# Two-layer graph network: A's last block by row tiles, W0's scale by slabs, bias added in PSUM, store in three parts

## What is computed

```python
# layer 0
h = jnp.maximum(_layernorm(x), 0.0)
hidden = h @ W0 + b0
x = x + (adj != 0) @ hidden / deg[:, None]     # deg: column sums of adj != 0
# layer 1, 4 heads of 512
h = jnp.maximum(_layernorm(x), 0.0)
ht = (h @ W1) by heads; src, dst = ht @ a_src, ht @ a_dst
e = leaky_relu(src[:, :, None] + dst[:, None, :]) + adj
x = x + (softmax(e) @ ht).mean over heads
```

## Time and profile before

| | us |
|---|---|
| median of 3 runs | 2520.13 (2519.99 to 2520.54) |
| the profiled execution | 2519.26 |
| its span | 2517.5 |
| TensorE busy in it | 2453.3 (97%) |
| VectorE busy | 1878.0 (75%) |
| ScalarE busy | 1260.7 (50%) |

### The profile page before, as it was taken

One profiled execution on the slowest core, in us unless ns is written; L12 is line 12 of the kernel. 1 busy time (PEld: TensorE's weight loads), 2 busy tenths in 40 slices (PEclk: granted clock), 3 DMA queues, 4 the chain that ended last, 5 costly groups with the idle time before them and its releaser, 6 DMA issues.

```text
span 2517.5 us, 42703 instructions
## 1 busy us (share of the span) xinstructions
PE 2453.3 (97%) x12304; PEld 1202.2 (48%) x12304; DVE 1878.0 (75%) x2570; ACT 1260.7 (50%) x1881; POOL 47.6 (2%) x42
## 2 busy tenths in 40 slices
PE   6999999799999999999999999999999999999997
PEld 3444446444444444444444444444444444444785
DVE  7788766776787766877668776687766886767775
ACT  4545645644455444554445544455445554444563
POOL 0000000000000000000000000000000000000000
PEclk9999999799999999999999999999999999999999
DMA  4186647100021000310003000030001200001000
GB/s 146 52 296 193 234 150 247 51 5 5 25 84 46 4 4 25 93 38 4 4 25 96 34 4 4 25 96 34 4 4 33 88 34 3 2 17 44 26 1 9
DMA packets 74148, 144.20 MB, mean 57 GB/s; under 512 B 4414, under 2 KB 11840, under 8 KB 72895
## 3 DMA queue, kind: packets, MB, share of 16 engines
q1 hardware_dynamic: 74047, 143.08, 17.7%
HBM read 129.37 MB, written 13.70 MB: 57 GB/s over the span
## 4 chain that ended last, share of the span: by engine, by line
PE 95%; DVE 2%; ACT 1%; issue 1%; DMA 1%; SPq 0%; ACTq 0%; DVEq 0%
PE z_ps L718 70%; PE o_ps L746 11%; PE z_ps L1326 6%; PE o_ps L1326 4%; PE c_ps L1326 1%; PE c_ps L1358 1%; PE o_ps L1299 1%; PE c_ps L1299 1%; PE o_ps L1350 0%; ACT h_reg L1155 0%; DVE w_reg L1001 0%; DMA row_reg<-b_in 0%; DVE bst L984 0%; PE o_ps L1286 0%; ACT w_reg L1162 0%
## 5 line engine op out<-in xcount | busy, mean ns | idle before, releaser
L718 PE MATMUL z_ps<-hl_reg,h_reg 128*128 (+2 forms) x8736 | 1758.5, 364 | 10.6 <-DVE hl_reg L595 10.6
L718 PEld LDWEIGHTS z_ps<-hl_reg,h_reg 128*128 (+1 forms) x8736 | 855.1, 98 | 910.5 <-DVE hl_reg L595 10.9
L546 ACT ACTIVATE hl_reg<-t_reg (+2 forms) x364 | 361.9, 994 | 729.3 <-DVE t_reg L622 379.3
L595 DVE TENSOR_TENSOR hl_reg<-t_reg,hl_reg (+2 forms) x364 | 417.4, 1147 | 234.5 <-ACT hl_reg L546 232.3
L531 ACT ACTIVATE t_reg<-ring_reg,vv 128x512 f32 (+3 forms) x728 | 526.4, 770 | 67.5 <-DVE ao_reg L610 60.7
L622 DVE SCALAR_TENSOR_TENSOR t_reg<-t_reg,vv,e_reg (+3 forms) x728 | 509.9, 741 | 10.7 <-issue 8.2
L610 DVE TENSOR_TENSOR ao_reg<-ao_reg,t_reg 128x1024 f32<-128x1024 f32 (+1 forms) x336 | 383.4, 1141 | 0.0
L746 PE MATMUL o_ps<-w_reg,z_reg 128*128 128x512 f16 x1248 | 278.2, 379 | 0.9 <-DVE z_reg L638 0.9
L746 PEld LDWEIGHTS o_ps<-w_reg,z_reg 128*128 128x128 f16 x1248 | 119.8, 98 | 140.9 <-DVE z_reg L638 1.2
L638 DVE SCALAR_TENSOR_TENSOR z_reg<-z_ps,z_reg 128x512 f16<-128x512 f32 (+1 forms) x112 | 73.2, 653 | 151.6 <-ACT z_reg L558 151.6
L445 ACT ACTIVATE e_reg<-e_reg (+2 forms) x91 | 90.3, 996 | 153.8 <-DVE e_reg L456 153.5
(11 more groups left out here) (153 smaller groups left out, 1055.2 us busy)
## 6 DMA issues: line engine op xcount, KB each, us to landing
ring_reg<-adjT_in SPq DMA_DIRECT2D x78, 512.0 KB, 4.7
e_reg<-adjT_in SPq DMA_DIRECT2D x78, 512.0 KB, 3.7
ring_reg<-x_in SPq DMA_DIRECT2D x13, 512.0 KB, 4.4
x_dram<-ring_reg SPq DMA_DIRECT2D x13, 512.0 KB, 6.4
ring_reg<-c_dram SPq DMA_DIRECT2D x24, 256.0 KB, 3.3
ao_reg<-x_dram SPq DMA_DIRECT2D x6, 1024.0 KB, 5.5
out_dram<-ao_reg SPq DMA_DIRECT2D x6, 1024.0 KB
w_reg<-W_in SPq DMA_DIRECT2D x5, 1024.0 KB, 6.0
```

What stands on the lines that cost most here:

```text
L546: nc.scalar.activation(hl_ring[:, g % HL_RING, 0, :, 0:W], t_ring[:, g % T_RING, :, 0:W], ACT.Copy).then_inc(hi_ready, 1)
L595: nc.vector.tensor_tensor(hl_ring[:, g % HL_RING, 1, :, 0:W], t_ring[:, g % T_RING, :, 0:W], hl_ring[:, g % HL_RING, 0, :, 0:W], ALU.subtr ...
L718: mm = nc.tensor.matmul(z_ps[:, k, 0:W], hk[hs], hl_ring[:, r, ps, u, 0:W], start=first and u == 0 and n == 0, stop=last and u == 1 and n ...
```

## The change

**Store.** The last block's 128 rows are stored as soon as their sum is done; of the other 127 rows, 112 and 15 are stored apart. **Bias.** b0 times the scale is split in two fp16 halves, high in partitions 0 to 63 and low in 64 to 127 of one tile; a 13th matmul a tile, against a constant tile (b0_one), adds it in PSUM. hid16's halves are made from PSUM; `hidden_sum` and its fp32 buffer go. **W0's scale.** x's first tile is loaded first (group 0 is one tile, the next three), then W0 in four slabs, each with its own maximum; one matmul of ones with the maxima gives every partition their sum, which takes the maximum's place as a scale (SH is 8 times larger for it). The lists of the head are written out anew. **A's last block.** It goes row tile by row tile: 13 pairs for the first row tile, then 13 for the second, and so on, 52 steps of 4 matmuls. All 13 A tiles live to the end of it; row_reg is taken out of the ring. At the steps LN1_AT (6, 8, 10, 11, 13 ... 46) stand one tile's transposes and the scores of the tile before, for 25 tiles; at steps 4, 10 and 16 the last groups of row maxima, at 24 their transposition, all before max_bc is loaded. The block's tiles are groups of two, one and one. Loads of e follow the a_pe counts of the fourth row tile. The fp16 splits of the last two pairs (`high1`, `split1`) stand behind c's transposition.

```diff
+ROW_SLOT = 10
...
+            if g == LAST0:
+                ring = [(r, q) for r, q in ring if r != ROW_SLOT]
...
+        LN1_AT = [math.ceil(6 + 5 * m / 3) for m in range(NT - 1)]
+        LATE_SPLIT = PAIRS - IT // 2
...
+        late_max = [3, 4, 5]
+        LATE_MAX_AT = [4, 10, 16]
+        MR_AT = 24
...
-                           else FULL * H * IT + H * LASTW // P + 2)
+                           else FULL * H * IT + H * LASTW // P + 1)
                 if isinstance(b, int) and b == FULL:
-                    r0 = FULL * BW
-                    sp.dma_start(out[r0:r0 + P, :], out_acc[:, 0]).then_inc(out_st, 16)
-                    sp.dma_start(out[r0 + P:N, :], out_acc[0:LASTP, 1]).then_inc(out_st, 16)
+                    r0, r1 = FULL * BW, FULL * BW + P
+                    sp.dma_start(out[r0:r1, :], out_acc[:, 0]).then_inc(out_st, 16)
+                    sp.wait_ge(o_out, FULL * H * IT + H * LASTW // P + 2)
+                    sp.dma_start(out[r1:r1 + LAST16, :], out_acc[0:LAST16, 1]).then_inc(out_st, 16)
+                    sp.dma_start(out[r1 + LAST16:N, :], out_acc[LAST16:LASTP, 1]).then_inc(out_st, 16)
...
-                sp.dma_start(w0_raw.rearrange("p (k n) -> p k n", k=KT),
-                             W0.rearrange("(k p) n -> p k n", p=P)).then_inc(w0_in, 16)
                 load_x(0)
+                for k in range(KT):
+                    sp.dma_start(w0_raw[:, k * D:(k + 1) * D], W0[k * P:(k + 1) * P, :]).then_inc(w0_in[k], 16)
...
-                for i in range(PAIRS):
+                for i in range(LATE_SPLIT):
                     store_x1(i)
...
-                    if i >= 2:
-                        sp.wait_ge(a_pe, LAST0 + i - 1)
-                        load_e(sp, 0, i - 2)
...
+                sp.wait_ge(mr_sb, 1)
+                sp.dma_start(max_dram.rearrange("(t i) -> t i", i=P), max_st[0:NT]).then_inc(mr_out, 16)
+                sp.wait_ge(mr_out, 16)
+                load_max(sp, 0)
+                for p in range(PAIRS):
                     sp.wait_ge(a_pe, LAST0 + p + 1)
                     load_e(sp, 0, p)
-                sp.wait_ge(mr_sb, 2)
-                sp.dma_start(max_dram[order[-1] * BW:FULL * BW].rearrange("(t i) -> t i", i=P),
-                             max_st[0:IT]).then_inc(mr_out, 16)
+                for i in range(LATE_SPLIT, PAIRS):
+                    store_x1(i)
...
+                def w0_maximum(k):
+                    dve.wait_ge(w0_in[k], 16)
+                    nc.vector.tensor_reduce(w0m[:, k:k + 1], w0_raw[:, k * D:(k + 1) * D], AX_X, ALU.max,
+                                            apply_absolute_value=True).then_inc(s_w0red, 1)
...
+                    dve.wait_ge(s_b0hi, 1)
+                    nc.vector.tensor_tensor(b0_16[P // 2:P], b0_bc[P // 2:P], b0_16[P // 2:P],
+                                            ALU.subtract).then_inc(s_b0lo, 1)
...
-                def hidden_sum(t):
...
-                    nc.vector.tensor_tensor(hid16[:, t, 1], hid32[:, t % 4], hid16[:, t, 0],
-                                            ALU.subtract).then_inc(hid_lo, 1)
+                    if t == NT - 1:
+                        dve.wait_ge(s_lastsc, 1)
+                    nc.vector.scalar_tensor_tensor(out=hid16[:, t, 1], in0=o_ps[:, 2] if t % 2 == 0 else c_ps[:],
+                                                   scalar=SH if t < NT - 1 else last_sc[:], in1=hid16[:, t, 0],
+                                                   op0=ALU.mult, op1=ALU.subtract).then_inc(hid_lo, 1)
...
+                stats0(0)
+                w0_maximum(0)
+                variances0(0)
+                w0_maximum(1)
+                scalars0(0)
+                w0_maximum(2)
+                w0_maximum(3)
+                b0_maximum()
+                stats0(1)
                 w0_scale()
-                for t in range(2, 4):
-                    stats0(t)
-                group0(1)
-                for k in range(KT):
-                    w0_lo(k)
                 b0_scale()
-                dve.wait_ge(s_const, 4)
-                for i in range(NT + 6):
+                transposed_lo(0)
+                w0_lo(0)
+                stats0(2)
+                w0_lo(1)
+                stats0(3)
+                w0_lo(2)
+                w0_lo(3)
...
+                    if c == NG1 - 1:
+                        for p in range(E_PRE0):
+                            subtract_max(dve, 0, p)
+                    for i in range(i0, i1, 2):
+                        for k in range(i, min(i + 2, i1)):
+                            x1_tile(k)
+                        for k in range(i, min(i + 2, i1)):
+                            x1_stats(k)
+                    ln_variances(dve, t0, t1, x1_bst, i1, s_mv1, i1)
+                    while split < min(i0 // 2, LATE_SPLIT):
+                        split1(split)
+                        split += 1
...
+                    act.wait_ge(hid_ps, t + 1)
+                    if t == NT - 1:
+                        act.wait_ge(s_lastsc, 1)
+                    nc.scalar.activation(hid16[:, t, 0], o_ps[:, 2] if t % 2 == 0 else c_ps[:], ACT.Copy,
+                                         scale=SH if t < NT - 1 else last_sc[:]).then_inc(hid_hi, 1)
...
+                def high1(j):
+                    p = pairs1[j]
+                    if j >= LATE_SPLIT:
+                        act.wait_ge(a_pe, NA)
+                    act.wait_ge(st1_ready, 2 * j + 2)
+                    nc.scalar.activation(h16[:, 2 * p:2 * p + 2, 0], ln1_stage[:, j % 2],
+                                         ACT.Copy).then_inc(hi1_done, 1)
...
+                for j in range(LATE_SPLIT, PAIRS):
+                    high1(j)
...
-                    mm.then_inc(hid_ps, 1)
-
-                pe.wait_ge(s_const, 4)
+                            nc.tensor.matmul(bank, ht0[:, t % 3, hs, k], w0_16[:, ws, k],
+                                             start=k == 0 and m == 0, stop=False)
+                    if t == 0:
+                        pe.wait_ge(s_b0lo, 1)
+                    nc.tensor.matmul(bank, b0_one, b0_16, start=False, stop=True).then_inc(hid_ps, 1)
+
+                pe.wait_ge(s_const, 6)
+                transpose0(0)
                 pe.wait_ge(s_w0mx, 1)
-                nc.tensor.transpose(z_ps[0:1, 0, 0:P], w0mx[:], ident[:]).then_inc(w0t_ps, 1)
-                pe.wait_ge(s_w0row, 1)
-                nc.tensor.matmul(z_ps[:, 1, 0:1], w0row, ones32[0:1], start=True, stop=True).then_inc(w0b_ps, 1)
-                for t in range(NT + 2):
+                nc.tensor.matmul(z_ps[:, 0, 0:1], ones_m, w0mx[:], start=True, stop=True).then_inc(w0b_ps, 1)
+                hidden(0)
...
+                def late_step(it, p):
+
+                    g = LAST0 + p
+                    pe.wait_ge(a_ready, g + 1)
+                    a = a_ring[a_slot[g]]
+                    for u in range(2):
+                        for s in range(2):
+                            mm = nc.tensor.matmul(acc0(NB - 1, it), a[:, u, it * P:(it + 1) * P],
+                                                  hid16[:, 2 * p + u, s], start=p == 0 and u == 0 and s == 0,
+                                                  stop=p == PAIRS - 1 and u == 1 and s == 1)
+                    if it == IT - 1:
+                        mm.then_inc(a_pe, 1)
+                    elif p == PAIRS - 1:
+                        mm.then_inc(o_ready, 1)
+
+                pe.wait_ge(o_sb, o_count(NB - 2))
+                for step in range(IT * PAIRS):
+                    late_step(*divmod(step, PAIRS))
+                    for c, at in zip(late_max, LATE_MAX_AT):
+                        if step == at:
+                            pe.wait_ge(o_sb, o_count(NB - 1))
+                            pe.wait_ge(mx_fold, NB)
+                            if c != late_max[0]:
+                                pe.wait_ge(mt_red, len(early_max) + late_max.index(c))
+                            transpose_max(c, o_ps[:, 2])
+                    if step == MR_AT:
+                        max_rows()
+                    for i in range(NT - 1):
+                        if step == LN1_AT[i]:
+                            transpose1(i)
+                            if i > 0:
+                                scores(i - 1)
+                scores(NT - 2)
```

More of the change, by code:

```diff
@@ L18 @@
+import math
 from contextlib import ExitStack
@@ L237, in gnn_kernel @@
         LAST0 = NA - PAIRS
-        groups0 = [(0, 2), (2, 4), (4, 8), (8, 14), (14, 20), (20, NT)]
-        groups1 = [(t, t + IT) for t in range(0, order[-1] * IT, IT)] + [(FULL * IT, NT),
-                                                                         (order[-1] * IT, FULL * IT)]
+        groups0 = [(0, 1), (1, 4), (4, 8), (8, 14), (14, 20), (20, NT)]
+        L0 = order[-1] * IT
+        groups1 = [(t, t + IT) for t in range(0, L0, IT)] + [(FULL * IT, NT), (L0, L0 + 2),
+                                                             (L0 + 2, L0 + 3), (L0 + 3, L0 + 4)]
```

(48 more changed lines are left out.)

207 lines of the change are left out of this document (64 added, 143 removed).

## The result

| | before | after |
|---|---|---|
| median of 4 runs | 2520.06 (2518.62 to 2520.54) | 2495.56 (2493.88 to 2497.17) |
| the profiled execution | 2519.26 | 2494.08 |
| its span | 2517.5 | 2492.3 |
| TensorE busy | 2453.3 | 2447.1 |
| VectorE busy | 1878.0 | 1866.4 |

Times in us. The ratio after to before is 0.9904, with a 95% interval of 0.9886 to 0.9921. Forecast were 2497.5, in a range of 2491 to 2504.

A forecast was written before the change was run, and what follows sets the result against it. The prediction took TensorE as the bound in the hidden features, A's earlier blocks and second layer as untouched. Store -11.8, head and bias -0.6, last block +4.8, behind it -14.7 sum to -22.3: forecast 2497.5 us, range 2491 to 2504.

The forecast's parts named there:

- Store: End of the kernel: 127 rows stored as 112 and 15 use several DMA engines instead of one, -11.8 us.
- Rival B: Last store: the last 15 rows sit on one engine, +3.2 us, 2500.7; chance 7%.
- Bias matmul: Hidden features: one more 512-column matmul a tile at 0.22 us, paid by 24 tiles because TensorE bounds the stage, +5.3 us.
- Head: Start of the kernel: W0's scale is ready earlier, so the fifth tile's transposes start at 29.7 instead of 36.1, -6.2 us.
- rival C: Head gives nothing: b0 or x(1) lands late, or VectorE's longer list eats the gain; +6.2 us, 2503.7; chance 12%.
- A's last block: More transposes, scores and maxima inside the block, and a wait of 1.9 us from 14 ring slots: ends 4.8 us later.
- Rival A: A's last block: the vector chain paces it, six groups give +7 us, 2504.5; chance 15%.
- Rival E: A's last block: TensorE's granted clock falls to 0.50 and stays, all 80 us give 2537; chance 2%.
- Rival D: ScalarE and VectorE quicker behind the block, and no wait of 1.9 us in it: -4 us, 2493.5; chance 10%.
- Behind the block: Between A's last block and the second layer: one tile's chain instead of four, exponentials starting earlier, -14.7 us.
- Just in time: Behind the block: VectorE's four subtractions and two splits, 7.4 us, end just in time for the second layer's first product.
- rival F: Bunched e loads hold the second layer, c's store and load queue behind 6.8 MB: +8 us, 2505.5; chance 3%.

The follow-up runs named there:

- Maxima earlier too: The changed kernel with late row tiles two steps later (LN1_AT) and VectorE's four early reductions of block maxima two pairs earlier (MAX_DVE): 2490.73 us, ratio 0.9885.
- the head alone: The kernel before with the new head and the bias in PSUM, but the old last block, tail and store: 2517.95 us, ratio 0.999.
- the two runs with later steps: The changed kernel with LN1_AT counted from 8 instead of 6, 2493.73 us; and that with VectorE's early maxima reductions two pairs earlier, 2490.73 us.

## Why the prediction was right, and which term was off

It was right: 2495.56 against 2497.5, and every part of the sum moved the time the way that was forecast. One term was off by more than half, and one wait was not in the sum. Term by term, by the profiled spans:

- **Store**, -11.8 forecast, -11.4 measured, in the old kernel alone as well. The end behind the issue takes 2.8 us, not 2.0, and the issue comes 0.4 sooner. Rival B falls with its price of +3.2; on how many engines the 15 rows lie, the runs don't tell.
- **Bias matmul**, +5.3 forecast. This is the term that failed. The step was "TensorE bounds this stage, so the 24 tiles from the third on pay". TensorE didn't: the ring of waits through `hidden_sum` did, at 3.17 us, and left it 0.13 us a tile, some 3 us in all. I took 2.72/12 for a matmul's time and 0.45 for the transposes, and so put the wait into TensorE's work. Between the fifth tile's transposes and A's start, 75.3 us became 77.3: +2.0. TensorE's own slack paid for the other 3 us. That the removal of the addition is worth nothing beside the new matmul, as the prediction has it, holds, but not for its reason: the addition was in the ring that paced the stage, and only the matmul's 0.22 makes TensorE the bound.
- **Head**, -6.2 forecast, -5.9 measured (36.01 to 30.09). The prediction's own two times, 36.1 and 29.7, lie 6.4 apart. The scale came 1.1 us later than forecast and the fifth tile only 0.4, so part of this agreement is luck. Head and bias -3.9 instead of -0.6; rival C, a head that gives nothing, falls.
- **A's last block**, +4.8 forecast, +3.2 measured. The wait before the first transposes was forecast at 1.9 and measured at 1.97, at 365.42 instead of 366.2 to 368.1, since the block began 2.7 us earlier. The 1.0 us for a clock that may fall was not needed in this execution (the stage's granted clock is 1.00), nor the 0.47 for a tile's transposes, which take 0.44 in the chain, 0.8 us less for 25 tiles. Rival A, a vector chain that paces the block, falls: no wait but that one in 78.9 us, though VectorE is busy 61.90. Rival E falls too, with the clock at 1.00 through the block (whether transposes count for the clock, no run here tells); its 2537 would stand for 80 us spent at 0.50, while a block that takes 160 us instead of 80 would end at 2577. Rival D falls with the wait of 1.97.
- **Behind the block**, -14.7 forecast, -14.8 measured. "Just in time" for VectorE's list was right by little: that list, and not store and load of c, is what ends last. The e loads, with the two stores of x1 behind them, kept the DMA engines full for over 8 us beyond the block's end, which the prediction had named as the sign of rival F. F's cost of 8 us didn't come all the same, since c's store, at 447.64, found them nearly idle: F falls, and its sign was badly chosen.

```profile
436.00:444.00 8.00, 3.65 (x18) 3.06 (x18) 2.84 (x11) 3.74 (x5) 0.00 (x0) 0.67 0.99 345
444.00:448.00 4.00, 0.46 (x1) 0.16 (x1) 3.23 (x11) 3.42 (x8) 0.40 (x1) 0.50 0.15 57
```

- **Not in the sum**: the wait of 1.0 us for the block maxima at 311.9. VectorE's reductions ended only 0.6 us ahead of TensorE before (314.24 to 314.84), behind an adjacency piece that lands, counted from A's start, 1.5 us later with the change. The runs tie this to the 13th matmul, not to the shorter head (see "Maxima earlier too"); the cause stays open. I had said that A's earlier blocks are untouched.

By the spans the sum was -22.3 and the measurement -25.2: 3.3 more gained at head and bias, 1.6 at the block and 0.1 behind it, less 1.2 in A's earlier blocks, 0.5 in the second layer and 0.4 at the store. The medians lie 24.5 apart. That the forecast is only 1.9 us off is in part luck: 5.0 us more gained than forecast stand against 2.1 lost elsewhere.

## What to carry to other kernels

A stage in which an engine is 99% busy may still be paced by others: compare the length of the same group of matmuls at the stage's end, where nothing is behind it, and in its middle, and read who stands in the chain of waits in the middle. Adding work to such an engine costs less than the work (0.07 us a tile here for 0.22), and removing a step of the loop gains something (0.14 a tile), but the two don't add up: whichever bound is left then paces the stage. Look also for places with a small margin, such as the 0.6 us here between VectorE's last reduction and TensorE's need of its bank: a load that comes 1.5 us later uses it up, and two places earlier in a list gave it back. And before a store at the end, factor its number of rows.

## What the hardware showed that I had not expected

Behind the same wait of 1.9 to 2.0 us the granted clock fell in some executions and not in others, in the block (0.51 and 0.50 in two profiles, 1.00 in five) and in the head (behind a wait of 1.9 us in the run with the maxima earlier and in the head alone, not in after); where it fell, it was for 3.4 us, which cost 1.7. I know of nothing in these profiles that tells the two cases apart. Where the wait was 0.23 us, in the two runs with later steps, no fall followed in the block. And in the tail 113 rows cost 9.2 us more than 126.
